# Five edge tiles of a GNN layer move from GpSimd's gathers to row-by-row gathers on ScalarE's DMA queue

## The reference

```python
h = maximum(layernorm(x), 0)                       # per node
r = silu(silu(edge_attr_8 @ W1 + b1) @ W2 + b2)    # per edge, 8 -> 64 -> 64
tpw = r @ W3 + b3                                  # per edge, 4 blocks of 8 x 8
m0 = ALPHA * (einsum(hs[src] * sh0, W00) + INV_SQRT3 * einsum(hv[src], sh1, W110))
m1 = ALPHA * (einsum(hs[src], sh1, W01) + einsum(hv[src] * sh0, W10))
agg = segment_sum(concat(m0, m1), dst, 100000) / sqrt(16)
out = x + h_self(Ws, Wv) + agg
```

## Time and profile before

| what | value |
|---|---|
| device time, three runs | 608.64, 609.14, 609.26 us (median 609.14) |
| the profiled execution: device time | 608.37 us |
| its span | 606.5 us |
| PE busy | 534.4 us (88%) |
| POOL busy | 486.6 us (80%) |
| DVE busy | 413.6 us (68%) |
| ACT busy | 408.6 us (67%) |
| mean granted TensorE clock | 0.79 of 2.4 GHz |

### The profile page before, as it was taken

The page is one execution under the profiler, slowest core; times in us unless marked ns, Lnnn a source line. Parts: engine busy times, 40 slices in busy tenths (PEclk is TensorE's granted clock), DMA queues, the critical chain, the costliest instruction groups (busy, mean ns, idle before and its releaser), DMA issues.

```text
span 606.5 us, 13459 instructions
## 1 busy us (share of the span) xinstructions
PE 534.4 (88%) x3230; PEld 428.2 (71%) x3255; DVE 413.6 (68%) x1147; ACT 408.6 (67%) x1219; POOL 486.6 (80%) x390
## 2 busy tenths in 40 slices
PE   5879989978878799999999999999999999899930
PEld 4768878877765687677777777777777777577830
DVE  4767967966784767768778776765887787756240
ACT  3425535644545958679889987886998899956710
POOL 6777777777777777888888888888888888888887
PEclk9859969998987856767788888866888888776555
DMA  4645656656631001222222222222222222222222
GB/s 130 194 116 173 187 155 182 173 173 168 185 119 23 15 13 14 10 11 11 11 10 12 11 10 10 11 11 10 11 11 10 11 11 10 11 10 11 11 9 9
DMA packets 53337, 34.43 MB, mean 57 GB/s; under 512 B 36918, under 2 KB 40728, under 8 KB 53272
## 3 DMA queue, kind: packets, MB, share of 16 engines
q0 software_dynamic: 34144, 6.27, 19.3%
q1 hardware_dynamic: 11958, 14.65, 8.4%
q10 hardware_dynamic: 7170, 12.81, 5.7%
HBM read 17.59 MB, written 16.08 MB: 56 GB/s over the span
## 4 chain that ended last, share of the span: by engine, by line
POOL 65%; issue 23%; PE 8%; ACT 2%; DVE 1%; DMA 1%; ACTq 0%; POOLq 0%; DVEq 0%
POOL out_dram L332 36%; POOL xg L319 29%; PE ps L712 3%; PE ps L715 1%; PE ps L661 1%; PE ps L644 1%; PE ps L674 1%; ACT dsq L486 1%; DMA out_dram<-sums,idx_i 1%; PE ps L656 1%; DMA src_all<-in_src_dram 0%; DVE msg L1038 0%; PE ps L639 0%; ACT eq L509 0%; DVE gvar L878 0%
## 5 line engine op out<-in xcount | busy, mean ns | idle before, releaser
L332 POOL DMA_INDIRECT out_dram<-sums,idx_i x196 | 306.8, 1566 | 59.8 <-issue 58.0
L319 POOL DMA_INDIRECT xg<-in_x_dram,src_all x185 | 178.8, 967 | 57.4 <-issue 56.1
L712 PE MATMUL ps<-msg,eq 128*128 128x32 f32 (+1 forms) x980 | 143.0, 299 | 10.5 <-DVE msg L1051 10.0
L712 PEld LDWEIGHTS ps<-msg,eq 128*128 128x128 f32 x980 | 139.7, 223 | 10.8 <-DVE msg L1051 10.1
L1017 DVE TENSOR_TENSOR prod<-ps,coef 128x256 f32<-128x256 f32 (+1 forms) x245 | 98.6, 468 | 18.8 <-PE ps L661 16.6
L486 ACT ACTIVATE dsq<-ps,dcol 128x512 f32<-128x512 f32 x196 | 87.6, 546 | 0.2 <-PE ps L674 0.2
L980 DVE SCALAR_TENSOR_TENSOR first<-sums,rank_max,dmt_all 128x4 f32<-128x4 f32 x49 | 10.9, 222 | 96.0 <-ACT sums L472 95.8
L661 PE MATMUL ps<-w3blk,x 64*128 64x256 f32 x392 | 74.6, 512 | 0.4 <-ACT dsq L486 0.4
L509 ACT ACTIVATE eq<-dsq,onecol 128x384 f32<-128x384 f32 x147 | 73.8, 528 | 0.0
L384 ACT ACTIVATE sqT<-ps 128x512 f32<-128x512 f32 (+2 forms) x50 | 29.3, 585 | 62.5 <-PE ps L600 62.2
L661 PEld LDWEIGHTS ps<-w3blk,x 64*128 64x128 f32 x392 | 44.7, 247 | 37.5 <-issue 32.5
(11 more groups left out here) (106 smaller groups left out, 840.0 us busy)
## 6 DMA issues: line engine op xcount, KB each, us to landing
xg<-in_x_dram SPq DMA_DIRECT2D x1320, 0.1 KB
xin<-in_x_dram SPq DMA_DIRECT2D x48, 256.0 KB, 2.8
out_dram<-oc ACTq DMA_DIRECT2D x48, 256.0 KB, 2.6
out_dram<-sums,idx_i POOLq DMA_INDIRECT x196, 3.1
xg<-in_x_dram,src_all POOLq DMA_INDIRECT x185, 2.5
er_all<-in_edge_attr_dram SPq DMA_DIRECT2D x1, 780.0 KB
sh_all<-in_edge_attr_dram SPq DMA_DIRECT2D x1, 390.0 KB
xin<-in_x_dram SPq DMA_DIRECT2D x1, 192.0 KB, 2.9
```

What stands on the lines that cost most here:

```text
L319: pool.indirect_dma_start(xg[:, t * D:(t + 1) * D], None, x, bass.IndirectOffsetOnAxis(ap=src_all[:, t:t + 1], axis=0)).then_inc(signal, 16)
L332: pool.indirect_dma_start(out, bass.IndirectOffsetOnAxis(ap=idx_i[:, k % NS, a:a + 1], axis=0), sums[:, k % NS, a * DR:a * DR + D], None, ...
L712: m = pe.matmul(psSUM[:, a * DR:a * DR + n], eq[:, k % 2, o:o + P], msg[:, k % 2, b, 0:n], start=(b == a), stop=(not carried and (b == a - ...
```

## The change

POOL gathers tiles 0 to 179 (G1 is 180, RT is 16). SyncE's queue keeps its 1320 rows (tiles 185 to 195, now from G2 = G1 + RA = 185). The five tiles between, 180 to 184, are gathered on ScalarE's queue: 640 rows, one DMA each, in groups of three, four or six between the activations of the edge stage, 17 a batch (one group of three less in the first half pass), from pass 0 until shortly before the end of pass 9, half 0 (all its groups but the last). Ahead of each 32 rows, ScalarE's queue loads 32 offsets into its registers, 20 times. To have the groups at fixed rows, the loop over passes 3 to 8 on ScalarE is written out. LATE_UNITS becomes 30, 30, 12 and 4 tiles; `gc`, `gsq` and the like shrink to 30 tiles, and `row_i` and `row_at` hold 16 tiles.

```diff
-    GT, RT = 10, 11
+    GT, RT, RA = 10, 16, 5
     G1 = T + 1 - RT
+    G2 = G1 + RA
...
-            late_rows = iter([(t, p) for t in range(G1, T + 1) for p in range(P if t < T else TAIL)])
+            late_rows = iter([(t, p) for t in range(G2, T + 1) for p in range(P if t < T else TAIL)])
...
+            rows_of_tiles = iter([(t, p) for t in range(G1, G2) for p in range(P)])
+            offsets = []
+
+            def gather_rows(count):
+
+                for t, p in itertools.islice(rows_of_tiles, count):
+                    if p % 32 == 0:
+                        o = (t - G1) * P + p
+                        _, offsets[:] = nc.values_load_multi_w_load_instructions(
+                            row_at[0:1, o:o + 32], engines=[mybir.EngineType.Activation], min_val=0, max_val=(N - 1) * D * 4,
+                            skip_runtime_bounds_check_because="src holds rows of x")
+                    act.dma_start(xg[p:p + 1, t * D:(t + 1) * D].bitcast(u8), x_bytes[:, ds(offsets[p % 32], D * 4)])\
+                       .then_inc(gathered_row[t - G1], 16)
...
                         act.activation(ceq[:, k % 2, o], csq[:, o], ACT.Relu, bias=onecol[:, :], scale=-4.0,
                                        accum_out=ccnt[:, (k - 1) % NS, a:a + 1])
+                if k >= 1:
+                    gather_rows(4)
...
                     if not (first and h == 0):
+                        gather_rows(3)
                         copy_sums(q - 1, kq - 1)
                     dst_square(q + 1, kq + 1)
+                    gather_rows(4)
...
                         dst_col(q + 3, kq + 3)
+                    gather_rows(3)
                     dst_equal(q + 1, kq + 1)
+                    gather_rows(3)
...
+                    gather_rows(3)
                     copy_sums(q, kq)
                     dst_square(q + 2, kq + 2)
+                    gather_rows(4)
...
                         dst_col(q + 4, kq + 4)
+                    gather_rows(3)
                     dst_equal(q + 2, kq + 2)
+                    gather_rows(3)
...
-            with act.Fori(3, PASSES - 3) as v:
-                edge_pass(v, False, False)
-            for v in range(PASSES - 3, PASSES):
+            for v in range(3, PASSES):
                 edge_pass(v, False, v == PASSES - 1, SCALED.get(v), CENTRED.get(v))
```

More of the change, by code:

```diff
@@ L215, in rows @@
             return ap[ds(r0, p * r), :].rearrange("(p r) d -> p (r d)", p=p), p, r * D
+        x_bytes = x.bitcast(u8).rearrange("n d -> (n d)").rearrange("(a n) -> a n", a=1)
         block = ctx.enter_context(nc.Block(no_gpsimd_drain=True))
@@ L277, in _ @@
             sp.dma_start(out[N:N + BT * P, :].rearrange("(p r) d -> p (r d)", p=P), spare0[:, :]).then_inc(s["spare_stored"], 16)
-            x_bytes = x.bitcast(u8).rearrange("n d -> (n d)").rearrange("(a n) -> a n", a=1)
-            late_rows = iter([(t, p) for t in range(G1, T + 1) for p in range(P if t < T else TAIL)])
+            late_rows = iter([(t, p) for t in range(G2, T + 1) for p in range(P if t < T else TAIL)])
             OF_ROWS = (RT - 1) * P + TAIL
@@ L515, in _ @@
                 store(c, c)
+            act.wait_ge(s["rows_at"], 1)
             mlp_in(0, 0)
```

## The result

The changed kernel takes 631.7 us (median of 4 runs, 629.9 to 638.0) against 609.1: ratio 1.040, 95% interval 1.034 to 1.045. That is **slower by 22.6 us**; 625 was forecast, with a range of 607 to 648. The profiled execution is the longest of the four, 637.97 us with a span of 636.2, so its sums are made against 637.97 - 608.37 = 29.6 us.

What follows compares the result with a forecast made beforehand. POOL's fixed work bounds the kernel, the others 4.6 us ahead. Last indices come 19 - 4 + 2 + 3 = 20 us later; less the margin the end moves +16 us, to 625 us, range 607 to 648.

Steps and rivals of the forecast that it cites:

- What bounds the kernel: POOL's queue of fixed work sets the end, the last indices 4.62 us ahead; five gathers removed save 6.27 us.
- The queue's price: ScalarE's queue: 0.323 us a row, 2.13 a load, 1.0 dispatch; 6.5 us a batch, 8.6 with a load.
- The pace: 30 middle batches: 8.0 us each instead of 7.37, so +19 us, bounds 7 and 37.
- A load batch is not made up by the next: Edge-stage batches: 1.05 us slack lies in each batch and can't be saved up over two; hence 8.0, not 7.6.
- The last rows: VectorE in pass 9 waits for ScalarE's last rows: 6 us late, half made up, +3 us (0 to 6).
- The rest: Batches 4 and 5 no longer wait for POOL, -4 us; early loads +2; the last ten batches stay.
- The signs: DMAs 0.23 us, loads 2.1; POOL waits 20 us or more; VectorE waits in pass 9; ScalarE's idle time is issue.
- All hidden: Rival: ScalarE's queue needs less than 7.4 us a batch, pace stays 7.37, time 602.9 us; chance 0.14.
- Near the floor: Rival: pace 7.6 us, late batches made up by quicker ones; 607 to 612 us; chance 0.06.
- nothing hidden: Rival: each row DMA or load waits until ScalarE's engine is empty, 5.5 us more for 38 batches; about 810 us; chance 0.04.
- The clock rival: Rival: TensorE idles more, half clock 70% of the time, pace 9.3 us, end 662 us; chance 0.10.
- The rule against the row: Skill: instructions can be queued while a control instruction executes, hiding rows; profile row: SyncE's DMAs start one after another. Forecast followed the row.

Runs made afterwards that it cites:

- e12: The kernel before, unchanged, profiled once more; ratio 0.9996, 607.7 us.
- e9: Changed kernel with 20 loads on ScalarE's queue but only one row DMA behind each, other 620 rows left out; ratio 0.9913 to the kernel before, 602.8 us.
- e1: Changed kernel with all 640 row DMAs but one load of offsets in place of 20; ratio 0.9996 to the kernel before, 821.8 us.
- e10: Changed kernel with 18 rows a batch and 80 loads of 8 offsets in place of 20 of 32; ratio 1.0741 to the kernel before, 652.9 us.
- e7: Changed kernel with three tiles instead of five on ScalarE's queue, 11 rows a batch, 12 loads; ratio 0.9995 to the kernel before.
- e4: Changed kernel with 18 rows a batch instead of 17, the last rows out in pass 8; ratio 1.0396 to the kernel before.
- e6: Changed kernel with one load in place of 20 and 18 rows a batch; ratio 1.0026 to the kernel before.
- e11: Changed kernel with two tiles on ScalarE's queue, 8 rows a batch, none directly ahead of a copy of sums, 8 loads; ratio 0.9968, 606.05 us against 607.79.
- e3: Changed kernel with neither loads nor rows on ScalarE's queue, POOL gathering 180 tiles; ratio 0.9932 to the kernel before.
- e8: Changed kernel with four tiles instead of five on ScalarE's queue, 15 rows a batch, 16 loads; ratio 1.0133 to the kernel before.

## Why the prediction was right, and where its sizes were off

- **What bounds the kernel.** Right. POOL's fixed work set the end, with a margin for the rest. The margin of 4.6 us was that of one execution; e12 has 9.5 at the same time. e9 shows POOL's five gathers to be worth 5 us (607.8 to 602.8) if nothing else changes, for the 6.27 forecast.
- **The queue's price.** The row was priced right from SyncE's queue (0.323 us; 0.322 on ScalarE). A load was mis-sized: 2.13 us was taken, but it is 2.24 and the DMA behind it costs 0.24 more. With 5.5 + 1.0 + 2.5 = 9.0 us in place of 8.6 the sum meets the 8.90 of the batch shown above. The 1.0 us of dispatch stayed an estimate that no run measured by itself.
- **The pace.** Forecast 8.0 us from 7.37, measured 8.62 from 7.43: this is the term that failed in size, 31 us instead of 19, still inside its bounds (7 to 37). The batches with a load took 9.2 us on average (14 of the 26), those without 8.0, where I had kept 7.37. Among the latter five took 6.7 to 6.8, at clocks between 0.74 and 1.00, near the queue's 6.5; the two at a clock of 0.50 took 10.8 and 11.4. TensorE's clock in the stretch was 0.73 against 0.82 before.
- **A load batch is not made up by the next.** Right in the main: behind a load a step could take 6.7 us (batch 20 to 21: 6.69), less than the 7.37 kept for it, but the two together still took over 15.5 us where two batches before took 14.9. Below 6.69 none went, where 6.25 was reached before.
- **The last rows.** The wait was as forecast (6.68 us for 6), but nothing of it was made up: 5.8 us in place of 3.
- **The rest.** Forecast -4 + 2 around the early batches, measured +1.3 at batch 9. "Stay" was forecast for the ten last batches; they were 6.6 us quicker, at a clock of 0.73 in place of 0.65. But e12 has the kernel before at 81.0 us and 0.74 there, so that neither is shown to be an effect of the change.
- **The sum.** 20 - 4.6 is 15.4, not 16. The median moved by 22.6 us and the profiled execution by 29.6. That the range holds is partly luck: in the profiled execution the pace alone is 12 us over its term, the early batches 3, batches 36 to 38 5, and the ten last batches happened to take 6.6 off.
- **The signs.** DMA and load durations, POOL's waits and VectorE's wait came as written. ScalarE's idle time ahead of `sums` was put down mostly to PE (31.2 us against 9.0 of issue), not to issue; the queue's hold shows ahead of `eq`, `x` and `erT` as well.
- **The rivals.** All hidden falls with the result. Its point of decision, 7.4 us of queue a batch, holds only in part: e9 (3.5 us of queue in a load batch) and e1 (17 rows, 6.5 us) lie under it and keep the pace, e10 above it loses, but e7 (7.0 us in a load batch) lies under it and has 7.89. Near the floor (607 to 612) falls, and so does nothing hidden: 632 and not 810 us. The clock rival is partly true: three of the 26 steps ran at a clock of 0.50 or 0.51 and took 10.8 to 11.4 us (before, one: 10.9), where it had 70% of the time at 10.2. What the clock's own share is, no run separates.
- **The rule against the row.** In the batch shown above no activation passes a row DMA that stands before it, although the engine is free and the data are there. So what the Trainium skill says under Sequencer Loop (Advanced Engine Details and Errata) does not hide such rows: these DMAs and the load keep the queue from handing out what stands behind them. Whether the page counts them among its control instructions is open; the measurement decides. The row was the right one to follow.

## What to carry to other kernels

An engine's DMA queue is a resource of its own with a budget per loop step: add up every DMA, load and dispatch in it, by durations of the same instructions on another queue, and compare with the step's length. Work above that budget costs, and nearly in full (the changed kernel, e4, e10). Work under it can be free (e9, e1, e6, e11), but is not always: e7 lay under it and lost 0.6 to 0.7 us a batch, since a long instruction in the queue also lets the engine behind it run dry. So look at the sum, and at how long the longest stretch without an instruction for the engine is. And where two engines run at nearly the same pace, read the margin between them first, in more than one execution: it says how much of a saving the other one lets through, and here it was 4.6 and 9.5 us in two executions of one kernel.

## What the runs showed of the hardware

- The first row DMA behind a load of offsets takes 0.46 us on ScalarE's queue, the others 0.23. On SyncE's queue it is 0.26, against 0.23 for the others.
- A load of 8 offsets takes 0.82 us and one of 32 takes 2.24 (medians 0.825 in e10 and 2.235 in the changed kernel). From these two, an estimate: 0.35 us fixed and 0.06 an offset, so that small loads are dearer by the offset.
- An activation does not pass a load or a row DMA that stands before it in ScalarE's queue: the engine goes on 0.05 to 0.12 us after the last row DMA (21 of 22 waits in the changed kernel).
- TensorE, kept waiting by ScalarE, was granted 0.73 in place of 0.82 of its clock between batches 9 and 35; e1 and e3, with the pace of 7.2, had 0.85.
- The same kernel before, in two executions of 608.37 us, took 89.7 us at a clock of 0.65 and 81.0 us at 0.74 for its last ten batches.
- On two chips the same kernel takes 822 us. In the profiles taken there (e1 to e8, not of the kernel before) TensorE is busy 28 to 34 of the first 236 us, in which POOL gathers, where it is busy 202 in the kernel before elsewhere; in e3 it is busy 43 of the next 64. The cause is open.
